# Dense matmuls on constants ahead of the first layer's transposes, and a joined preparation of the masked self-attention

## The reference

```
x = layer0(x)   # rms norm; 16 heads of width 64; a causal window of 64 keys inside its segment
                # plus 32 extra keys (16 of memory, 16 persistent); gated feed-forward
x = layer1(x)   # cross-attention to the 6404 context rows, 16 heads of width 8; gelu feed-forward
x = layer2(x)   # cross-attention, residual, layer norm
x = layer3(x)   # masked self-attention over 1024 rows (16 heads of width 8), cross-attention, relu feed-forward
attn = softmax(q @ k.T * scale + mask); out = attn @ v @ Wo
```

## Time and profile before

| | before |
|---|---|
| median of 3 runs | 4127.81 us (4118.31 to 4130.98) |
| the profiled execution | 4127.73 us |
| its span, first to last instruction | 4125.9 us |
| PE busy | 3625.4 us, 88% of the span |
| DVE busy | 3426.0 us, 83% |
| ACT busy | 2805.1 us, 68% |
| POOL busy | 229.5 us, 6% |
| mean granted TensorE clock | 0.921 |

### The profile page before, as it was taken

How to read it: one execution, slowest core, us unless ns; L and a number is a source line. 1 busy time by engine, 2 the same in 40 slices (tenths; PEclk the granted TensorE clock), 3 DMA queues, 4 the chain that set the end, 5 groups by cost and what they waited for, 6 DMA issues and landing times. The chain is left out here.

```text
span 4125.9 us, 85445 instructions
## 1 busy us (share of the span) xinstructions
PE 3625.4 (88%) x35156; PEld 1229.0 (30%) x35156; DVE 3426.0 (83%) x3302; ACT 2805.1 (68%) x4037; POOL 229.5 (6%) x196
## 2 busy tenths in 40 slices
PE   5676799999999968999999998199859999999997
PEld 2353322222222232222222222045422222222222
DVE  4323899999999749999999995399969999999982
ACT  0332388888888826888888886145517888888885
POOL 3000000000000000000000000244400000000000
PEclk9657699999999978999999999599958999999998
DMA  3102111111111121111011102300011111111100
GB/s 103 48 1 52 25 26 18 29 29 17 28 29 17 52 55 27 18 29 29 15 29 29 22 10 72 60 5 6 3 31 35 26 19 29 29 15 29 29 3 8
DMA packets 57924, 117.54 MB, mean 28 GB/s; under 512 B 11458, under 2 KB 48514, under 8 KB 52290
## 3 DMA queue, kind: packets, MB, share of 16 engines
q1 hardware_dynamic: 54980, 110.19, 14.7%
q10 hardware_dynamic: 2592, 2.36, 0.2%
HBM read 84.95 MB, written 27.47 MB: 27 GB/s over the span
## 5 line engine op out<-in xcount | busy, mean ns | idle before, releaser
L1807 DVE TENSOR_REDUCE chunk_max<-max_scores 128x2 f32<-128x988 f32 (+1 forms) x2496 | 2787.3, 1178 | 122.1 <-PE max_scores L1655 83.4
L1786 ACT ACTIVATE probs<-scores 128x512 f32<-128x512 f32 (+1 forms) x3231 | 2453.2, 808 | 458.5 <-PE scores L1681 433.5
L1708 PE MATMUL values_sum<-probs,values 128*9 128x256 f32 x19584 | 1367.4, 381 | 0.0
L1681 PE MATMUL scores<-queries,key_ring 49*128 49x512 bf16 x4800 | 1226.3, 384 | 44.4 <-ACT probs L1786 12.1
L1655 PE MATMUL max_scores<-key_ring,queries 48*128 48x494 bf16 (+1 forms) x4992 | 979.5, 391 | 159.2 <-DVE chunk_max L1807 106.3
L1708 PEld LDWEIGHTS values_sum<-probs,values 128*9 128x9 f32 x19584 | 374.6, 89 | 757.5 <-issue 570.0
L1681 PEld LDWEIGHTS scores<-queries,key_ring 49*128 49x128 bf16 x4800 | 305.2, 94 | 635.8 <-ACT probs L1786 546.7
L1655 PEld LDWEIGHTS max_scores<-key_ring,queries 48*128 48x128 bf16 x4992 | 240.2, 94 | 851.3 <-DVE chunk_max L1807 529.4
L1341 ACT ACTIVATE probs<-scores 128x512 f32<-128x512 f32 x256 | 138.5, 592 | 106.2 <-PE scores L1293 106.2
L1367 DVE TENSOR_REDUCE chunk_max<-max_scores 128x1024 f32 (+1 forms) x128 | 154.9, 1213 | 23.0 <-PE max_scores L1249 22.9
L1759 ACT ACTIVATE values<-scores 128x512 f32<-128x512 f32 (+2 forms) x45 | 25.1, 565 | 208.2 <-PE scores L1665 195.4
(11 more groups left out here) (200 smaller groups left out, 1621.5 us busy)
## 6 DMA issues: line engine op xcount, KB each, us to landing
key_ring<-k_parts SPq DMA_DIRECT2D x96, 300.2 KB
key_ring<-k_parts SPq DMA_DIRECT2D x96, 200.1 KB
key_ring<-k_parts SPq DMA_DIRECT2D x96, 100.1 KB
k_parts<-queries SPq DMA_DIRECT2D x72, 128.0 KB, 2.4
o_whole<-values_sum_s SPq DMA_DIRECT2D x45, 128.0 KB, 8.3
k_parts<-k_part SPq DMA_DIRECT2D x36, 128.0 KB, 2.4
queries<-q_rows SPq DMA_DIRECT2D x6, 672.0 KB, 8.6
context<-in_ctx_t SPq DMA_DIRECT2D x1, 3202.0 KB, 17.3
```

What stands on the lines that cost most here:

```text
L1681: return pe.matmul(sc[:, g % 3, :], keys(rows, h, P * t, P * (t + 1)), qb[rows, q], start=True, stop=True)
L1708: mm = pe.matmul(acc[32 * b:32 * b + WV, 0:QBLOCK], vb[rows, h, t, :], pr[rows, slot, QBLOCK * (b % 2):QBLOCK * (b % 2 + 1)], start=(t == ...
L1786: act.activation(pr[:, a % RING:a % RING + b - a, :], sc[:, a % 3:a % 3 + b - a, :], ACT.Exp)\
L1807: dve.tensor_reduce(mx[:, h % 2, c, :, j], mxb[:, w % 2, :, 0:width], AX.X, ALU.max)\
```

## The change

In `windowed_attention` every `turn` gets, behind its waits and ahead of its transposes, eight bf16 matmuls with 256 moving columns on constants (`k.ident_b`, and `k.mean_w` read as bf16), whose result goes into the left half of the bank `pt_own`; the transposes overwrite it. On VectorE `normalise_pair(s - 1)` moves ahead of `mask_and_maximum(s)`.

The phases ahead of the self-attention are joined. `clear_self_rows` goes, and GpSimd does its two memsets in the first of the two layer norms, ahead of the mask. `load_first_keys` for the next cross-attention goes, and SP issues its DMAs inside `self_attention`, behind the loads of the first three heads. `query_terms` uses the form of the cross-attentions (`q_rows`, stores by SP and ScalarE) and issues four loads of `qb` (`whole`), which count into a new semaphore `self_rows`; it doesn't wait for them. `key_value_terms` has no loads of queries any more, and waits for `self_rows` at its end. The reduction `any_key` moves from the end of VectorE's list in `key_value_terms` to the start of its list in `self_attention`.

```diff
@@ windowed_attention, turn @@
                 pe.wait_ge(probs_odd, p + 1)
                 if n >= 1:
                     pe.wait_ge(turned_copied, 2 * n)
+                for _ in range(8):
+                    pe.matmul(pt_own[:, 0:2 * P], k.ident_b[:], k.mean_w[:].bitcast(BF16), start=True, stop=True)
                 for t in range(4):
                     pe.transpose(pt_own[:, P * t:P * (t + 1)], pn[:, p % 2, 4 * c + t, 0, :], k.ident[:])
@@ windowed_attention, VectorE @@
                 if s >= 3:
                     pair_out(s - 3)
+                if 1 <= s <= NPAIR:
+                    normalise_pair(s - 1)
                 if s < NPAIR:
                     mask_and_maximum(s)
-                if 1 <= s <= NPAIR:
-                    normalise_pair(s - 1)
@@ query_terms, SP @@
-                if q_rows is None:
-                    sp.dma_start(q_parts[:, p], part[p][:]).then_inc(stored, 16)
-                    continue
                 store_query_rows(sp, q_rows, part, p, 0, stored)
-            sp.wait_ge(stored, 16 * (NPART if q_rows is None else 2 * NTERM))
-            if q_rows is not None:
+            sp.wait_ge(stored, 16 * 2 * NTERM)
+            if whole:
+                for lo, hi in ((0, 2), (2, H)):
+                    for half in range(2):
+                        sp.dma_start(rows_of[1:1 + KROWS, N * lo:N * hi].rearrange("r (h c n) -> r c h n", c=2, n=HALF)[:, half],
+                                     q_rows[half, :, lo:hi]).then_inc(rest_fetched, 16)
+            else:
...
@@ key_value_terms, SP @@
-            for p in range(NPART):
-                for r in range(K_RUNS[p]):
-                    row = RUN_ROW[p] + HD * r
-                    sp.dma_start(qb[row:row + HD, :].rearrange("r (h n) -> r h n", h=H),
-                                 q_parts[:, p].rearrange("h d n -> d h n")).then_inc(fetched, 16)
...
-            sp.wait_ge(fetched, 16 * NTERM)
+            sp.wait_ge(k.self_rows, 64)
@@ key_value_terms, VectorE @@
-            if beside_vector is not None:
-                beside_vector(dve)
@@ self_attention, SP @@
                 load(h, h * nk)
                 sp.wait_ge(keys_loaded, KEY_DMAS * (h + 1))
+            for h in range(2):
+                load_keys(k, sp, h, 1, next_k_parts, k.first_keys[2])
@@ self_attention, VectorE @@
+            dve.tensor_reduce(any_key[:], mask_bytes[:], AX.X, ALU.max)
             for i in range(ni):
                 for u in range(TPI):
                     take_max(TPI * i + u, 0, i, u)
@@ program @@
                 def work(pool):
+                    if name == "mask_qk":
+                        pool.memset(qb[:].bitcast(F32), 0.0)
+                        pool.memset(kb[0:1, 0:KRING * N].bitcast(F32), PAIR_OF_ONES)
                     pool.wait_ge(k.arrived[name], 16)
...
-            clear_self_rows(k, kb, qb)
-            load_first_keys(k, 2, 1, k_parts[2])
-            query_terms(k, hn, k.w["L3_xattn_sa_wq"], v["L3_xattn_sa_bq"], q_parts)
+            query_terms(k, hn, k.w["L3_xattn_sa_wq"], v["L3_xattn_sa_bq"], q_rows, qb, k.self_rows, whole=True)
```

More of the change, by code:

```diff
@@ L96, in __init__ @@
         self.steps = 0
+        self.self_rows = ctx.enter_context(nc.semaphore("self_rows"))
         self.rest_rows = [ctx.enter_context(nc.semaphore(f"rest_rows_{n}")) for n in range(3)]
@@ L901, in gated_ffn, with query_terms @@
                                                       in1=cols(k.x, n), op0=ALU.add, op1=ALU.add))
-def query_terms(k, src, w, bias, q_parts, q_rows=None, rows_of=None, rest_fetched=None):
+def query_terms(k, src, w, bias, q_rows, rows_of, rest_fetched, whole=False):
     nc = k.nc
@@ L935, in _ @@
                 act.activation(cols(part[1], c), cols(rest, c), ACT.Copy).then_inc(middle, 1)
-            if q_rows is not None:
-                for p, ready in enumerate((high, middle, low)):
-                    act.wait_ge(ready, 2)
-                    store_query_rows(act, q_rows, part, p, 1, stored)
+            for p, ready in enumerate((high, middle, low)):
+                act.wait_ge(ready, 2)
+                store_query_rows(act, q_rows, part, p, 1, stored)
         @block.vector
@@ L985, in load_query_rows, with key_value_terms @@
                         q_rows[half, :, lo:hi].rearrange("r h n -> r (h n)"))
-def key_value_terms(k, src, tk, ni, wk, bk, wv, bv_row, k_parts, vb, qb, q_parts,
-                    beside_vector=None):
+def key_value_terms(k, src, tk, ni, wk, bk, wv, bv_row, k_parts, vb):
     nc = k.nc
@@ L1017, in key_value_terms @@
         bias_loaded = sem("bias_loaded")
-        fetched = sem("fetched")
         stored = [sem("stored") for _ in range(NPART)]
@@ L1140, in restore_ones, with self_attention @@
     return work
[L1143 to L1157, removed]
+def self_attention(k, tk, ni, kb, qb, vb, k_parts, o_raw, mask, mask_bytes, any_key, next_k_parts):
     nc = k.nc
@@ L1908, in program @@
         k = Core(nc, ctx)
-        q_parts = nc.dram_tensor("q_parts", [H, NPART, HD, N], BF16).ap()
         q_rows = nc.dram_tensor("q_rows", [2, KROWS, H, HALF], BF16).ap()
@@ L1926, in attend @@
                 vb = scope_tools(k, c2)[0]("values", [P, H, NTILE, WV])
-                query_terms(k, src, k.w[prefix + w[0]], bq, None, q_rows, qb, k.rest_rows[layer])
+                query_terms(k, src, k.w[prefix + w[0]], bq, q_rows, qb, k.rest_rows[layer])
                 cross_attention(k, layer, base, qb, vb, k_parts[layer], o_whole, k.w[prefix + w[1]], k.w[prefix + w[2]],
@@ L1965, in program @@
             o_raw = s2("o_raw", [P, H * QT * VC])
-            clear_self_rows(k, kb, qb)
-            load_first_keys(k, 2, 1, k_parts[2])
-            query_terms(k, hn, k.w["L3_xattn_sa_wq"], v["L3_xattn_sa_bq"], q_parts)
+            query_terms(k, hn, k.w["L3_xattn_sa_wq"], v["L3_xattn_sa_bq"], q_rows, qb, k.self_rows, whole=True)
             key_value_terms(k, hn, P, 2, k.w["L3_xattn_sa_wk"], v["L3_xattn_sa_bk"], k.w["L3_xattn_sa_wv"],
-                            d["bv_sa"], k_self, vb, qb, q_parts,
-                            beside_vector=lambda dve: dve.tensor_reduce(any_key[:], bytes_qk[:], AX.X, ALU.max))
-            self_attention(k, P, 2, kb, qb, vb, k_self, o_raw, (m_qk, m_kq))
+                            d["bv_sa"], k_self, vb)
+            self_attention(k, P, 2, kb, qb, vb, k_self, o_raw, (m_qk, m_kq), bytes_qk, any_key, k_parts[2])
             normalised_output(k, o_raw, o_t, any_key)
```

## The result

The changed kernel takes 4058.81 us (median; 4057.51 to 4067.11) against 4126.95 us: ratio 0.9842, 95% interval 0.9821 to 0.9863, a gain of 68 us. The forecast was 4060. The execution that was profiled is the slowest of the four, 4067.11 us with a span of 4065.3; its stages together are therefore some 8 us above the median. Its mean clock is 0.933, that of the three others 0.937 to 0.938.

What follows compares the result with a forecast made beforehand. It saw a first-layer attention loop of 20.53 us a pair at clock 0.50, TensorE waiting 4.6, and a chain of waiting phases into the self-attention. 4127.73 less 34 (attention) and 34 (join) is 4060; range 4034 to 4093.

Steps and rivals of the forecast that it cites:

- The wait for the exponentials ahead of the mask: First layer's attention: VectorE, with normalisation first, waits for the previous pair's exponentials ahead of the mask; costed at nothing.
- The rival that they are dear: Dense matmuls cost as much as f32 ones of 512 columns, 0.94 us each; total 4186, chance of slower 0.02.
- halfway: First layer's attention: about half the stretch at full clock, between gains of 7 and 61, so 34 us.
- The alternation: First layer's attention: the granted clock switches between both levels, expected from 190 to 310 us.
- The sum for the full clock: First layer's attention at full clock: maximum, exponentials, copies, TensorE's work; 12.1 us a pair, gain of 61 us.
- up nearly throughout: Rival: full clock through nearly all the first layer's attention, gain 61 us, total 4033; chance 0.18.
- the rival's 20: Rival: stores and loads slower than in the cross-attentions, so the join gives 20 us, total 4074; chance 0.09.
- (a): Way into self-attention: without clearing and first-key phases the query projection comes 1.0 us behind the norm; gain 14.2 us.
- (b): Way into self-attention: query projection to key projection takes 15.1 us in place of 24.5; gain 9.4 us.
- (d): Start of self-attention: `any_key`, 8.67 us, now stands ahead of the first maximum; cost 4 us.
- The clearing beside the first norm: GpSimd's memsets beside the first norm, 15.3 us with the mask; cost taken as 0, or ending 2.9 us late.
- (c): Way into self-attention: key projection to first score matmul takes 22.1 us in place of 36.7; gain 14.6 us.

Runs made afterwards that it cites:

- e5_way_mended: Changed kernel with GpSimd's mask pass in eight pieces, the bias loaded at the head of `query_terms`, and `any_key` in two halves: 4043.23 us.
- e1_no_dense: Changed kernel without its 128 dense matmuls, VectorE's new order and the joined way kept: 4067.5 us.
- e4_join_only: Kernel before with the joined way into the self-attention alone, old VectorE order, no dense matmuls: 4101.83 us, ratio 0.9948.
- e6_scalar_order: Changed kernel with ScalarE's copies of the first half's transposes ahead of the next pair's exponentials: 4041.16 us.
- e9_scalar_order_transposes: Changed kernel with ScalarE's copies ahead of the next pair's exponentials, and eight transposes of the identity in place of the dense matmuls: 4045.82 us.
- e7_scalar_order_no_dense: Changed kernel with ScalarE's copies ahead of the next pair's exponentials and without the dense matmuls: median 4060.65 us, executions from 4036.4 to 4073.0.
- e11_both_two: Changed kernel with the edits of e5_way_mended and e6_scalar_order, and two dense matmuls a turn in place of eight: 4027.41 us.

## Why the prediction was right, and where not

The median is within 2 us of the forecast, and part of that is luck. In the profiled execution stage 1 gains 38.6 us where 34 was forecast, the join 27.9 where 34 was, and the other stages lose 6 where nothing was: 7 us over the forecast together. The three other executions are 7 to 10 us faster; in which stage isn't shown. The same code of stage 1 took 126.2 in `e5_way_mended`, a gain of 46.2, so the miss there can be larger than the profile says.

One reading of the prediction is wrong: the slices of the first layer's attention are the second to the fourth of the earlier trace rows, not the fifth, and of the two behind the 25th only the 26th belongs to the joined way. No number of the sum came from them.

**VectorE's order.** The first dense matmul stands at 189.01; 189.1 was forecast. The 4.5 us of idleness are gone, as said. The wait for the exponentials ahead of the mask costs nothing, as said. `e1_no_dense` against `e4_join_only`, 34 us, is what this part is worth, where the prediction had some 28 at the low clock.

**The dense matmuls** cost 1.66 us a turn at the low clock and 0.9 at the full one; 1.7 and 0.9 were forecast. The rival that they are dear falls.

**The clock** was the open question, and halfway (34 us) came near to the 38.6. Halfway was a choice between two computed ends, so its nearness is luck. The alternation is there, but its cause with the dense matmuls in place, which the prediction didn't find, is ScalarE's list: the first copies stand behind eight exponentials of the next pair, and `e6_scalar_order`, which puts them ahead, has the full clock through the loop. The sum for the full clock named that chain (maximum, eight exponentials, two copies, 12.1 us) as the bound and didn't draw the conclusion that an exchange of the two takes it away. With the exchange stage 1 gains 62.4 us; the rival "up nearly throughout" had 61. One term in it was wrong: TensorE's own work doesn't halve. Scores go from 3.95 us a half (189.57 to 193.52 above) to 2.47 (198.28 to 200.75), values from 2.1 to 1.2, so a pair with dense work is 11.1 and not 9.7. The rival's time came out all the same, because the chain of 12.1 that it had as the bound is gone there, and TensorE's 11.1 bounds.

**The extra transposes.** The Trainium skill ("TensorE: Matmul & The Clock Gate", Part 4) says that transposes don't count as busy for the full clock. `e9_scalar_order_transposes` has 1.00 with extra transposes, and four executions within 2.6 us, where the profiled execution of `e7_scalar_order_no_dense`, without them, has 0.50. By that the rule doesn't hold here. Two things stay open. The trace writes these transposes as MATMUL, so whether they run in the mode that the page means isn't shown. And why the loop without them stays low in some executions and not in others (4036.4) isn't settled by these runs.

**The join** (the joined way into the self-attention), 34 forecast, 27.9 measured on the way, 21 by the ratio of `e4_join_only`, which is below the forecast's lower end of 24 and as near to the rival's 20. (a) came out: 1.0 us behind the norm. (b) too: 15.4 for 15.1. (d) too: `any_key` holds the first maximum by 3.7, forecast 4. The first score matmul stands 35 us earlier relative to the norm's end, where 38 was to show it right. Two terms failed:

- The clearing beside the first norm was costed at 0, with 2.9 at most. The norm grew from 17.9 to 21.7 us, 3.8. I had looked at when GpSimd is through, not at what runs beside it: the mask pass, now behind the memsets, falls on VectorE's product. A row of before showed a trace of it, a product that took 1.45 us (2578.41, below). The Trainium skill ("SBUF — State Buffer", SBUF: two separate sides) states the mechanism: a VectorE operation with two SBUF inputs and a GpSimd operation that reads SBUF exclude each other for a whole instruction. The trace agrees, with 5.26 us for a pass in one piece and 1.50 for pieces; the reciprocal beside the same pass keeps its 3.35. By that rule the term could have been had from rows of before: if the clearing and the pass (15.3 us) start with the norm, at 2567.85, they end at 2583.2, and the product's start at 2578.41 is 4.7 us ahead of that; less the 0.8 that it lost before, 4 us.

```profile
2567.85 3.75 PE L283 MATMUL mean<-x,mean_w 128*128 128x512 f32 x4 [5.32 <-PEq L354]
...
2578.41 1.45 DVE L311 TENSOR_TENSOR t<-t,t 128x512 f32<-128x512 f32 x1
```

- (c), 22.1 forecast, 25.1 measured. The prediction allowed 5 us for the bias behind the row loads and left it out of the sum. The bias addition comes 11.2 us after the key projection, before 8.5, so it cost 3 there; this is one of the signs that the prediction named as showing it wrong. 18.5 in `e5_way_mended` shows 6 to 7 to be had.

All other stages together are 6 us longer in the profiled execution, no stage by more than 1.4. Nothing in the change that I know of accounts for it. `e5_way_mended` has 1 us by the same count, so it isn't the change's as a whole.

## What to carry to other kernels

When a wait is taken out of a loop, write down the next one by instruction and see which engine's list makes it; here two lines of ScalarE's order were worth a quarter of the whole change's gain. Before work goes to an idle GpSimd, look at which VectorE instructions run beside it, not only at when it ends, and cut a long pass into pieces. And a filler that holds the clock is judged by the spread of the executions, not by one: without it the same loop ran at 4036 and at 4073.

## What the runs showed of the hardware

- A TensorE that the profile counts as busy without a gap can stay at the low clock: 20.00 of 20 us at 0.50, four stretches in a row, in the profiled execution of `e7_scalar_order_no_dense`.
- Eight transposes of a constant raise the clock as well as eight dense bf16 matmuls of 256 columns (1.00 and 1.00 from 210 to 250 in `e9_scalar_order_transposes` and `e6_scalar_order`); with two of these it comes later (0.91 and 1.00 there in `e11_both_two`).
- A half's f32 scores, of 64 and 32 columns on parts of the array, gain a factor of 1.6 from twice the clock (3.95 to 2.47 us).
- Beside one GpSimd pass of 7.02 us a VectorE product of 0.69 took 5.26; beside eight pieces, 9.45 us together, it took 1.50.
